# Edge attention: who normalises the four row tiles of a group, VectorE and GpSimd or VectorE alone

## The chip, the cores and the metric

The kernel runs on one core of a Trainium2 chip. The time is that of the device for the whole program, in microseconds (us). The core's engines work side by side, each through its own list of instructions in order, and hand over by semaphores: TensorE multiplies and transposes, VectorE and ScalarE work on rows in the on-chip memories SBUF and PSUM, GpSimd does elementwise work on SBUF, and SyncE issues the DMAs.

## The reference

A network of four layers over 128 graphs of 64 nodes with 256 features, each of the form x + layer(relu(layernorm(x))): graph convolutions with LSTMs over windows, an attention over 512 edges, a two-stage convolution with batch norm, a dense attention. The change lies in the second, the attention over edges. What it computes, cut:

```python
h = maximum(layernorm(x, axis=-1), 0)                 # (128, 64, 256), eps 1e-5
Xq = (h @ W_lin.T).reshape(bt, n, heads, dh)          # 4 heads of 64
Xv = (h @ W_val.T).reshape(bt, n, heads, dh)
e = einsum('behd,hd->beh', leaky_relu(Xq[:, src] + Xq[:, dst], 0.2), a)
e = e + log(adj[src, dst] + 1e-8)
attn = softmax of e over the edges with the same src
Y = segment_sum(attn[..., None] * Xv[:, dst], src)
x = x + Y @ W_out.T
```

The layernorm's first step is what the change touches: (x - mean) * (variance + eps) ** -0.5 for each row.

## The kernel before

The 8192 rows (graph and node) lie on 128 partitions in 16 groups of 4 row tiles of 128 rows each (GT = 4). `edge_attention` (L940) handles them in 4 quarters of 4 groups; q counts quarters, m groups in one, and G = 4q + m is the group's number, 0 to 15. Each engine's program is written out by hand in the order of a common schedule: `group(q, m)` has 8 steps i, one for each graph of group m, and in them the work for the next group (`project`, `split_hi`, `split_lo`) and for the one after that, n = m + 2, is done ahead: the transposes back to rows (`turn_back`, i = 0), x1 = x + h (`add_x`), the statistics (`measure`, i = 0, and `moments`, i = 1), the normalisation (`normalise`, i = 3), the transposes of the normalised rows (`turn`, i = 5). The code for quarter 0 is unrolled, the middle two are a loop, the last is cut short. Groups 0, 1 and 2 are prepared in the opening and in `group(0, 0)`.

The normalisation before the change: VectorE leaves mean and variance of every row in c_mv and variance + eps in c_ve (L1496, semaphore var_eps). GpSimd takes that to the power -0.5 (L1092, c_rstd, semaphore rstd_ready). Then VectorE normalises the tiles 0 and 1 (NT = 2) with one tensor_scalar each (L1503), and GpSimd the tiles 2 and 3 with a subtraction (L1096) and a multiplication (L1099) over both. Each adds one to the semaphore normed, and TensorE's `turn` (L1154) waits for both. In the trace these rows are named l_w and x1 is l_x. The last thing in VectorE's step 3, behind `normalise`, is `split_lo` (L1532, L1535), which copies the values and writes the low halves of c_keys out of the PSUM bank c_pU; TensorE may write the next projection (`project`, L53 to L55) into c_pU only then. Beside that, `gather` (L1193) and `score` (L1208) are TensorE's other work in a group.

GpSimd has a second task in this phase: `make_pairs` (L1106) multiplies the one-hot tables of sources and destinations into edge_pairs, in eight instructions of 2048 elements for each partition. Three stand behind group 2's share of the normalisation, once VectorE has made the tables (`one_hot_columns`, L1719 and L1720, just ahead of `normalise(0, 2)`), and five behind group 3's. VectorE's `edge_cuts` (L1707 to L1710) stands in step 6 of `group(0, 0)`, after the first three are under way.

Of the kernel before, what the change touches and what calls it, by code (L numbers as in the profile page):

```python
# [8 lines left out]
ALU = mybir.AluOpType  # L9
# [3 lines left out]
P = 128  # L13
BATCH, NODES, D = 128, 64, 256
# [3 lines left out]
GT = 4  # L18
# [20 lines left out]
def wait(eng, sem, value):  # L39

    if isinstance(value, int) and value <= 0:
        return
    eng.wait_ge(sem, value)
# [896 lines left out]
def edge_attention(core, x, x2, tables, h_rows, spilled, pairs, late):  # L940


    nc = core.nc
    NQ, QG, QT = 4, 32, 16
    GG = GT * TILE_GRAPHS
    NJ = QT // GT
    AHEAD = 2
    HG = GG // 2
    NH = QG // HG
    NT = 2  # L950
    with ExitStack() as ctx:
        sb, ps = allocator(nc, ctx)
        tab = tables.tab
# [2 lines left out]
        xt, hst, landed = late.x, late.w, late.landed  # L956
        st, mv, ve, rstd = sb("c_st", [P, GT, 6]), sb("c_mv", [P, GT, 2]), sb("c_ve", [P, GT]), sb("c_rstd", [P, GT])
# [38 lines left out]
        sem = {n: core.sem("c_" + n) for n in names}  # L996
# [23 lines left out]
        with nc.Block() as block:  # L1020
# [62 lines left out]
            @block.gpsimd  # L1083
            def _(pool):
                nc.gpsimd.memset(mhalf[:, :], -0.5).then_inc(sem["half_set"], 1)
                nc.gpsimd.memset(lin[:, :], 0.0).then_inc(sem["half_set"], 1)
                pool.wait_ge(sem["half_set"], 2)

                def normalise(q, m):
                    G = NJ * q + m  # L1090
                    pool.wait_ge(sem["var_eps"], G + 1)
                    nc.gpsimd.tensor_tensor(rstd[:, :], ve[:, :], mhalf[:, :], ALU.pow).then_inc(sem["rstd_ready"], 1)  # L1092
                    pool.wait_ge(sem["rstd_ready"], 2 * G + 1)
                    xn = hst[m % 2][:, :, :].rearrange("p k (a d) -> p (k a) d", d=D)
                    shape = [P, GT - NT, D]
                    nc.gpsimd.tensor_tensor(xn[:, NT:, :], xt[m % 2][:, NT:, :],  # L1096
                                            mv[:, NT:, 0:1].to_broadcast(shape), ALU.subtract).then_inc(sem["rstd_ready"], 1)
                    pool.wait_ge(sem["rstd_ready"], 2 * G + 2)
                    nc.gpsimd.tensor_tensor(xn[:, NT:, :], xn[:, NT:, :], rstd[:, NT:].unsqueeze(2).to_broadcast(shape),  # L1099
                                            ALU.mult).then_inc(sem["normed"], 1)  # L1100

                def make_pairs(first, end):
                    for n in range(first, end):
                        c, half = n // 2, slice(n % 2 * NODES // 2, (n % 2 + 1) * NODES // 2)
                        shape = [P, NODES // 2, NODES]
                        nc.gpsimd.tensor_tensor(pairs[:, c, :].rearrange("p (i j) -> p i j", j=NODES)[:, half, :],  # L1106
                                                tab["src"][:, c, half].unsqueeze(2).to_broadcast(shape),
                                                tab["dst"][:, c, :].unsqueeze(1).to_broadcast(shape),
                                                ALU.mult).then_inc(sem["pairs_made"], 1)

                def body(q, last=False):
                    for m in range(3, NJ if last else NJ + 3):
                        normalise(q, m)
                        if isinstance(q, int) and q == 0 and m == 3:
                            make_pairs(3, NP)

                normalise(0, 0)
                normalise(0, 1)
                normalise(0, 2)
                pool.wait_ge(spilled[0], 16)  # L1120
                pool.wait_ge(spilled[1], 16 * (SPILLS - 1))
                pool.wait_ge(tables.made, ONE_HOT)
                make_pairs(0, 3)
                body(0)
                with pool.Fori(1, NQ - 1) as q:
                    body(q)
                body(NQ - 1, last=True)
                pool.wait_ge(late.opened["var_eps"], 1)
                nc.gpsimd.tensor_tensor(late.rs[:, :], late.ve[:, :], mhalf[:, :], ALU.pow).then_inc(late.opened["rstd_ready"], 1)

            @block.tensor
            def _(pe):
# [14 lines left out]

                def turn(q, m):

                    pe.wait_ge(sem["normed"], 2 * (NJ * q + m + 1))  # L1150
                    xn = hst[m % 2][:, :, :].rearrange("p k (a d) -> p (k a) d", d=D)
                    for t in range(GT):
                        for k in range(KD):
                            last = nc.tensor.transpose(pT[:, k, t * P:(t + 1) * P], xn[:, t, k * P:(k + 1) * P],  # L1154
                                                       tab["ident"][:, :])
                    last.then_inc(sem["t2"], 1)
# [312 lines left out]
            def _(dve):  # L1469
# [8 lines left out]
                def measure(q, m):  # L1478
                    G = NJ * q + m
                    dve.wait_ge(sem["x1_done"], G + 1)  # L1480
                    wait(dve, sem["rstd_ready"], 2 * G)
                    V.memset(ve[:, :], EPS)
                    for t in range(GT):
                        last = V.bn_stats(st[:, t, :], xt[m % 2][:, t, :])
                    last.then_inc(sem["stats"], 1)

                def moments(q, m):
                    G = NJ * q + m
                    dve.wait_ge(sem["stats"], 2 * G + 1)
                    wait(dve, sem["normed"], 2 * G)  # L1490
                    V.memset(unused[:, :], 0.0)
                    for t in range(GT):
                        last = V.bn_aggr(mv[:, t, :], st[:, t, :])
                    last.then_inc(sem["stats"], 1)
                    dve.wait_ge(sem["stats"], 2 * G + 2)
                    V.tensor_tensor(ve[:, :], ve[:, :], mv[:, :, 1], ALU.add).then_inc(sem["var_eps"], 1)  # L1496

                def normalise(q, m):
                    G = NJ * q + m
                    dve.wait_ge(sem["rstd_ready"], 2 * G + 1)  # L1500
                    xn = hst[m % 2][:, :, :].rearrange("p k (a d) -> p (k a) d", d=D)
                    for t in range(NT):
                        last = V.tensor_scalar(xn[:, t, :], xt[m % 2][:, t, :], mv[:, t, 0:1],  # L1503
                                               rstd[:, t:t + 1], ALU.subtract, ALU.mult)
                    last.then_inc(sem["normed"], 1)
# [244 lines left out]
def attention_layer(core, x, x2, h_rows, spilled, pairs, tables, late):  # L1750
    with ExitStack() as ctx:
        sb, _ = allocator(core.nc, ctx)
        sb("t_tables", [P, Tables.BYTES // 4])
        edge_attention(core, x, x2, tables, h_rows, spilled, pairs, late)
# [839 lines left out]
```

## Time and profile before

| | us |
|---|---|
| median of three runs | 2063.58 |
| lowest and highest | 2061.97, 2063.68 |
| span of the profiled execution | 2060.7 |
| TensorE busy | 1967.9 |
| VectorE busy | 1255.3 |
| ScalarE busy | 1000.0 |
| GpSimd busy | 224.2 |

Of the profiled execution the span from the first to the last instruction is known; its own device time isn't listed apart from the three runs. An engine's busy time is the sum of its instructions' durations. The names of tiles are those of the program: c_ for the edge attention, t_ for its tables, l_ for buffers that later phases share. A group that reads "x2" stands for two instructions, with the time from the start of the first to the end of the second; in brackets stands how long the engine had been idle before, and which instruction ended that.

### The profile page before, as it was taken

How to read it: one execution, taken by the hardware profiler on the slowest of the kernel's cores; microseconds unless marked ns; L12 is line 12 of the kernel's file. 1: busy time of each engine (PE TensorE's matmuls, PEld its weight loads, DVE VectorE, ACT ScalarE, POOL GpSimd, SP SyncE). 2: the span in 40 equal slices, each digit the busy share in tenths (PEclk: the TensorE clock that was granted, in tenths of full speed). 3: DMA queues.
4: the chain of work that ended last, by engine and by line, in shares of the span. 5: the costliest groups of instructions: out<-in, count | busy, mean ns of one | idle time of the engine just before them, and what ended most of it. 6: DMA issues, size and time to landing. Idle time of an engine off the chain costs nothing. (4 is left out here: it accounts for less than half of the span.)

```text
span 2060.7 us, 33850 instructions
## 1 busy us (share of the span) xinstructions
PE 1967.9 (95%) x12438; PEld 1632.4 (79%) x12438; DVE 1255.3 (61%) x2629; ACT 1000.0 (49%) x1675; POOL 224.2 (11%) x202
## 2 busy tenths in 40 slices
PE   6999999999999999999999889999999899897998
PEld 6998888888899999888888556757566688686998
DVE  7454665454455545555653776565664488897786
ACT  2554664333333433323332464462636246575996
POOL 1000000100110111011011350010100011100000
PEclk9999999999999999999999999999999999998999
DMA  3101001000100000101002321422314032001232
GB/s 118 56 27 41 0 0 41 0 0 0 41 1 0 0 0 0 31 1 41 41 0 82 133 72 52 145 83 85 112 36 151 12 113 71 23 0 52 82 103 92
DMA packets 81486, 99.92 MB, mean 48 GB/s; under 512 B 7408, under 2 KB 73584, under 8 KB 79088
## 3 DMA queue, kind: packets, MB, share of 16 engines
q1 hardware_dynamic: 81392, 98.65, 14.6%
q8 instruction: 61, 1.00, 0.2%
q14 instruction: 33, 0.27, 0.0%
HBM read 61.78 MB, written 33.55 MB: 46 GB/s over the span
## 5 line engine op out<-in xcount | busy, mean ns | idle before, releaser
L703 ACT ACTIVATE b_gate<-b_pG,b_bias 128x512 f32<-128x512 f32 (+1 forms) x504 | 303.9, 633 | 356.5 <-PE b_pG L55 355.6
L53 PE MATMUL b_pG<-b_xshi,b_whi 128*128 128x512 f32 (+1 forms) x1008 | 366.7, 364 | 2.2 <-PEq L299 1.4
L55 PE MATMUL b_pG<-b_xshi,b_wlo 128*128 128x512 f32 (+1 forms) x1008 | 366.1, 363 | 0.0
L54 PE MATMUL b_pG<-b_xslo,b_whi 128*128 128x512 f32 (+1 forms) x1008 | 366.1, 363 | 0.0
L753 DVE CAST b_xshi<-HT 128x512 fp32r<-128x512 f32 (+3 forms) x142 | 58.9, 457 | 284.4 <-PE b_pG L55 267.7
L53 PEld LDWEIGHTS b_pG<-b_xshi,b_whi 128*128 128x128 f32 x1008 | 189.2, 188 | 29.2 <-issue 3.5
L54 PEld LDWEIGHTS b_pG<-b_xslo,b_whi 128*128 128x128 f32 x1008 | 189.2, 188 | 25.7
L55 PEld LDWEIGHTS b_pG<-b_xshi,b_wlo 128*128 128x128 f32 x1008 | 189.2, 188 | 25.4
L55 PE MATMUL b_pG<-b_hshi,b_wlo 128*128 128x512 f32 (+1 forms) x576 | 205.1, 356 | 0.0
L54 PE MATMUL b_pG<-b_hslo,b_whi 128*128 128x512 f32 (+1 forms) x576 | 205.1, 356 | 0.0
L53 PE MATMUL b_pG<-b_hshi,b_whi 128*128 128x512 f32 (+1 forms) x576 | 205.1, 356 | 0.0
L711 ACT ACTIVATE b_tc<-b_cell 128x512 f32<-128x512 f32 (+1 forms) x144 | 83.7, 581 | 213.6 <-DVE b_cell L897 111.7
L724 POOL TENSOR_TENSOR b_gate<-b_gate 128x512 f32<-128x512 f32 (+1 forms) x72 | 83.2, 1156 | 924.6 <-ACT b_gate L703 924.6
L1400 ACT ACTIVATE c_relu<-c_pZ 128x512 f32<-128x512 f32 x256 | 138.3, 596 | 37.4 <-PE c_pZ L1193 36.3
L53 PEld LDWEIGHTS b_pG<-b_hshi,b_whi 128*128 128x128 f32 x576 | 108.1, 188 | 12.6
L54 PEld LDWEIGHTS b_pG<-b_hslo,b_whi 128*128 128x128 f32 x576 | 108.1, 188 | 12.5
L55 PEld LDWEIGHTS b_pG<-b_hshi,b_wlo 128*128 128x128 f32 x576 | 108.1, 188 | 12.3
L757 DVE TENSOR_TENSOR b_xslo<-HT,b_xshi 128x512 fp32r<-128x512 f32 (+1 forms) x142 | 100.1, 746 | 2.4
L901 DVE TENSOR_TENSOR HT<-b_gate,b_tc 128x512 f32 (+3 forms) x72 | 51.8, 720 | 66.5 <-ACT b_tc L711 66.5
L1193 PE MATMUL c_pZ<-t_both,c_keys 128*128 128x512 f32 x256 | 86.9, 423 | 0.0
L1193 PEld LDWEIGHTS c_pZ<-t_both,c_keys 128*128 128x128 f32 x256 | 42.1, 188 | 46.8 <-issue 33.5
L904 DVE TENSOR_TENSOR b_tc<-b_gate,b_tc 128x512 f32<-128x512 f32 (+1 forms) x72 | 44.0, 611 | 54.7 <-ACT b_tc L711 54.7
(366 smaller groups left out, 3975.8 us busy)
## 6 DMA issues: line engine op xcount, KB each, us to landing
a_xt<-in_x SPq DMA_DIRECT2D x16, 512.0 KB, 5.6
h_scratch<-HT SPq DMA_DIRECT2D x4, 2048.0 KB, 7.6
l_x<-in_x SPq DMA_DIRECT2D x16, 512.0 KB, 4.0
l_w<-h_scratch SPq DMA_DIRECT2D x16, 512.0 KB, 5.1
x_scratch<-l_x SPq DMA_DIRECT2D x16, 512.0 KB, 3.2
c_x<-x_scratch SPq DMA_DIRECT2D x32, 256.0 KB, 3.9
x_scratch<-c_x SPq DMA_DIRECT2D x32, 256.0 KB, 2.9
l_x<-x_scratch SPq DMA_DIRECT2D x16, 512.0 KB, 3.8
```

The source lines that it names most:

```text
L53: nc.tensor.matmul(out, w_hi, x_hi, start=first, stop=False)
L54: nc.tensor.matmul(out, w_hi, x_lo, start=False, stop=False)
L55: return nc.tensor.matmul(out, w_lo, x_hi, start=False, stop=last)
L703: nc.scalar.activation(gate[s][:, g, 0:plan.n], pG[s][:, g, 0:plan.n], SIG[g], bias=bias[:, plan.p - 1, 2 * g + s:2 * g + s + 1])\
L711: nc.scalar.activation(tc[s][:, 0:plan.n], cell[b][:, s, 0:plan.n], ACT.Tanh).then_inc(tanh_ready, 1)
L724: nc.gpsimd.tensor_tensor(gate[s][:, I, 0:plan.n], gate[s][:, I, 0:plan.n], gate[s][:, G, 0:plan.n], ALU.mult).then_inc(ig_ready, 1)
L753: nc.vector.tensor_copy(plan.flat(xs_hi[b][:, k, :]), plan.windows(it, b, k, t))\
L757: last = nc.vector.tensor_tensor(plan.flat(xs_lo[b][:, k, :]), plan.windows(it, b, k, t), plan.flat(f32(xs_hi[b][:, k, :])), ALU.subtract)
L901: nc.vector.tensor_tensor(plan.windows(it, b, s, t), plan.flat(gate[s][:, O, :]), plan.flat(tc[s][:, :]), ALU.mult).then_inc(h_ready, 1)
L904: nc.vector.tensor_tensor(tc[s][:, 0:n], gate[s][:, O, 0:n], tc[s][:, 0:n], ALU.mult).then_inc(h_ready, 1)
L1193: nc.tensor.matmul(pZ[i % 2][:, k, :], keys[:, i, k * P:(k + 1) * P], tab["both"][:, :], start=True, stop=True).then_inc(sem["z_mm"], 1)
L1400: nc.scalar.activation(relu_rows[i % RB][:, k, :], pZ[i % 2][:, k, :], ACT.Relu).then_inc(sem["r_done"], 1)
```

## The change

All four tiles are normalised by VectorE, with four tensor_scalar instructions in place of two. GpSimd keeps the power alone; its subtraction and multiplication (2 x 16 instructions) go. The counts of the semaphores are adapted: normed and rstd_ready rise by one for each group instead of two. GpSimd's function gets one more wait, for the rows of the group before (normed), since the power overwrites c_rstd, which the normalisation reads.

```diff
--- before.py
+++ after.py
@@ -947,7 +947,6 @@
     AHEAD = 2
     HG = GG // 2
     NH = QG // HG
-    NT = 2
     with ExitStack() as ctx:
         sb, ps = allocator(nc, ctx)
         tab = tables.tab
@@ -1086,18 +1085,11 @@
                 nc.gpsimd.memset(lin[:, :], 0.0).then_inc(sem["half_set"], 1)
                 pool.wait_ge(sem["half_set"], 2)
 
-                def normalise(q, m):
+                def root(q, m):
                     G = NJ * q + m
                     pool.wait_ge(sem["var_eps"], G + 1)
+                    wait(pool, sem["normed"], G)
                     nc.gpsimd.tensor_tensor(rstd[:, :], ve[:, :], mhalf[:, :], ALU.pow).then_inc(sem["rstd_ready"], 1)
-                    pool.wait_ge(sem["rstd_ready"], 2 * G + 1)
-                    xn = hst[m % 2][:, :, :].rearrange("p k (a d) -> p (k a) d", d=D)
-                    shape = [P, GT - NT, D]
-                    nc.gpsimd.tensor_tensor(xn[:, NT:, :], xt[m % 2][:, NT:, :],
-                                            mv[:, NT:, 0:1].to_broadcast(shape), ALU.subtract).then_inc(sem["rstd_ready"], 1)
-                    pool.wait_ge(sem["rstd_ready"], 2 * G + 2)
-                    nc.gpsimd.tensor_tensor(xn[:, NT:, :], xn[:, NT:, :], rstd[:, NT:].unsqueeze(2).to_broadcast(shape),
-                                            ALU.mult).then_inc(sem["normed"], 1)
 
                 def make_pairs(first, end):
                     for n in range(first, end):
@@ -1110,13 +1102,13 @@
 
                 def body(q, last=False):
                     for m in range(3, NJ if last else NJ + 3):
-                        normalise(q, m)
+                        root(q, m)
                         if isinstance(q, int) and q == 0 and m == 3:
                             make_pairs(3, NP)
 
-                normalise(0, 0)
-                normalise(0, 1)
-                normalise(0, 2)
+                root(0, 0)
+                root(0, 1)
+                root(0, 2)
                 pool.wait_ge(spilled[0], 16)
                 pool.wait_ge(spilled[1], 16 * (SPILLS - 1))
                 pool.wait_ge(tables.made, ONE_HOT)
@@ -1147,7 +1139,7 @@
 
                 def turn(q, m):
 
-                    pe.wait_ge(sem["normed"], 2 * (NJ * q + m + 1))
+                    pe.wait_ge(sem["normed"], NJ * q + m + 1)
                     xn = hst[m % 2][:, :, :].rearrange("p k (a d) -> p (k a) d", d=D)
                     for t in range(GT):
                         for k in range(KD):
@@ -1478,7 +1470,7 @@
                 def measure(q, m):
                     G = NJ * q + m
                     dve.wait_ge(sem["x1_done"], G + 1)
-                    wait(dve, sem["rstd_ready"], 2 * G)
+                    wait(dve, sem["rstd_ready"], G)
                     V.memset(ve[:, :], EPS)
                     for t in range(GT):
                         last = V.bn_stats(st[:, t, :], xt[m % 2][:, t, :])
@@ -1487,7 +1479,7 @@
                 def moments(q, m):
                     G = NJ * q + m
                     dve.wait_ge(sem["stats"], 2 * G + 1)
-                    wait(dve, sem["normed"], 2 * G)
+                    wait(dve, sem["normed"], G)
                     V.memset(unused[:, :], 0.0)
                     for t in range(GT):
                         last = V.bn_aggr(mv[:, t, :], st[:, t, :])
@@ -1497,9 +1489,9 @@
 
                 def normalise(q, m):
                     G = NJ * q + m
-                    dve.wait_ge(sem["rstd_ready"], 2 * G + 1)
+                    dve.wait_ge(sem["rstd_ready"], G + 1)
                     xn = hst[m % 2][:, :, :].rearrange("p k (a d) -> p (k a) d", d=D)
-                    for t in range(NT):
+                    for t in range(GT):
                         last = V.tensor_scalar(xn[:, t, :], xt[m % 2][:, t, :], mv[:, t, 0:1],
                                                rstd[:, t:t + 1], ALU.subtract, ALU.mult)
                     last.then_inc(sem["normed"], 1)
```

On GpSimd, at the place where the pairs are made (between the powers of group 2, group 3 and group 4). Before:

```order
L1092 TENSOR_TENSOR c_rstd<-c_ve,c_mhalf 128x4 [waits c_var_eps]
L1096 TENSOR_TENSOR l_w_52<-l_x_50,c_mv 128x512 [waits c_rstd_ready]
L1099 TENSOR_TENSOR l_w_52<-l_w_52,c_rstd 128x512 [waits c_rstd_ready]
L1106 TENSOR_TENSOR edge_pairs<-t_src,t_dst 128x2048 [waits t_made,h_spilled_rest,h_spilled_first]
L1106 TENSOR_TENSOR edge_pairs<-t_src,t_dst 128x2048 x2
L1092 TENSOR_TENSOR c_rstd<-c_ve,c_mhalf 128x4 [waits c_var_eps]
L1096 TENSOR_TENSOR l_w_53<-l_x_51,c_mv 128x512 [waits c_rstd_ready]
L1099 TENSOR_TENSOR l_w_53<-l_w_53,c_rstd 128x512 [waits c_rstd_ready]
L1106 TENSOR_TENSOR edge_pairs<-t_src,t_dst 128x2048 x5
```

Now, with the powers of groups 1 and 2 ahead and those of groups 4 to 6 behind:

```order
L1092 TENSOR_TENSOR c_rstd<-c_ve,c_mhalf 128x4 [waits c_normed,c_var_eps] x2
L1098 TENSOR_TENSOR edge_pairs<-t_src,t_dst 128x2048 [waits t_made,h_spilled_rest,h_spilled_first]
L1098 TENSOR_TENSOR edge_pairs<-t_src,t_dst 128x2048 x2
L1092 TENSOR_TENSOR c_rstd<-c_ve,c_mhalf 128x4 [waits c_normed,c_var_eps]
L1098 TENSOR_TENSOR edge_pairs<-t_src,t_dst 128x2048 x5
L1092 TENSOR_TENSOR c_rstd<-c_ve,c_mhalf 128x4 [waits c_normed,c_var_eps] x3
```

The pairs stand directly behind a power, and the five of the second batch have no wait of their own.

On VectorE, from the last one-hot tables to the end of step 3 of `group(0, 0)`, with group 2's normalisation. Before:

```order
L1719 TENSOR_SCALAR t_src<-s_iota_row,s_s_col 128x64
L1720 TENSOR_SCALAR t_dst<-s_iota_row,s_d_col 128x64
L1503 TENSOR_SCALAR l_w_52<-l_x_50,c_mv,c_rstd 128x256 [waits c_rstd_ready]
L1503 TENSOR_SCALAR l_w_52<-l_x_50,c_mv,c_rstd 128x256
L1532 COPY c_vals<-c_pU 128x256 [waits c_s_hi]
L1535 TENSOR_TENSOR c_keys<-c_pU,c_keys 64x256 x2
```

Now:

```order
L1711 TENSOR_SCALAR t_src<-s_iota_row,s_s_col 128x64
L1712 TENSOR_SCALAR t_dst<-s_iota_row,s_d_col 128x64
L1495 TENSOR_SCALAR l_w_52<-l_x_50,c_mv,c_rstd 128x256 [waits c_rstd_ready]
L1495 TENSOR_SCALAR l_w_52<-l_x_50,c_mv,c_rstd 128x256 x3
L1524 COPY c_vals<-c_pU 128x256 [waits c_s_hi]
L1527 TENSOR_TENSOR c_keys<-c_pU,c_keys 64x256 x2
```

Four instructions with one wait ahead of them stand where two stood; what follows is the same.

## Rows read from the trace of the kernel before

**Rows 1.** The page: the span, and TensorE's busy time, weight loads apart.

```profile
span 2060.7 us, 33850 instructions
PE 1967.9 (95%) x12438; PEld 1632.4 (79%) x12438; DVE 1255.3 (61%) x2629; ACT 1000.0 (49%) x1675; POOL 224.2 (11%) x202
```

**Rows 2.** A window: stretch, its us, PE busy (instructions), granted clock, DMA share, GB/s.

```profile
1160.00:1600.00 440.00, 416.01 (x3628) 1.00 0.28 91
```

**Rows 3.** PE's waits, 1130 to 1680: for whom, total us, times, longest us.

```profile
PE c_pT L1154 <- DVE l_w L1503: 9.7, 15, 2.7
```

**Rows 4.** The timeline of a regular group: start us, us, engine, line, operation.

```profile
1338.43 1.01 POOL L1092 TENSOR_TENSOR c_rstd<-c_ve,c_mhalf 128x4 f32<-128x4 f32 x1 [15.67 <-DVE c_ve L1496]
...
1339.47 2.35 DVE L1503 TENSOR_SCALAR l_w<-l_x,c_mv,c_rstd 128x256 f32<-128x256 f32 x2 [1.12 <-POOL c_rstd L1092]
...
1339.52 1.04 POOL L1096 TENSOR_TENSOR l_w<-l_x,c_mv 128x512 f32<-128x512 f32 x1
...
1340.63 1.04 POOL L1099 TENSOR_TENSOR l_w<-l_w,c_rstd 128x512 f32<-128x512 f32 x1
...
1340.83 0.73 PE L1193 MATMUL c_pZ<-t_both,c_keys 128*128 128x512 f32 x2
...
1341.88 1.09 PE L1154 MATMUL c_pT<-t_ident,l_w 128*128 128x128 f32 x8 [0.31 <-DVE l_w L1503]
...
1343.21 0.50 PE L53 MATMUL c_pU<-t_wqv_hi,c_hThi 128*128 128x512 f32 x1 [0.23 <-DVE c_keys L1535]
```

**Rows 5.** The timeline of group 0's normalisation, with GpSimd idle beside it.

```profile
1146.34 0.74 DVE L1503 TENSOR_SCALAR l_w<-l_x,c_mv,c_rstd 128x256 f32<-128x256 f32 x2
...
1146.67 0.41 DVE L1503 TENSOR_SCALAR l_w<-l_x,c_mv,c_rstd 128x256 f32<-128x256 f32 x1
```

**Rows 6.** The timeline: TensorE where it waits for nothing.

```profile
1188.43 0.71 PE L1193 MATMUL c_pZ<-t_both,c_keys 128*128 128x512 f32 x2
...
1202.05 0.74 PE L1193 MATMUL c_pZ<-t_both,c_keys 128*128 128x512 f32 x2
1202.63 0.40 PE L53 MATMUL c_pU<-t_wqv_hi,c_hThi 128*128 128x512 f32 x1
```

**Rows 7.** The timeline: transposes of a group with a softmax scan, one of three.

```profile
1257.60 1.09 PE L1154 MATMUL c_pT<-t_ident,l_w 128*128 128x128 f32 x8 [1.19 <-DVE l_w L1503]
```

**Rows 8.** The timeline: the pairs on GpSimd, and VectorE's instructions beside them.

```profile
1175.50 7.26 POOL L1106 TENSOR_TENSOR edge_pairs<-t_src,t_dst 128x2048 fp32r<-128x2048 f32 x2
...
1180.92 2.38 DVE L1709 TENSOR_TENSOR t_cut<-c_work 128x511 f32<-128x511 f32 x1
...
1182.72 4.06 POOL L1106 TENSOR_TENSOR edge_pairs<-t_src,t_dst 128x2048 fp32r<-128x2048 f32 x1
...
1183.34 3.73 DVE L1710 TENSOR_SCALAR t_cut<-t_cut 128x513 f32<-128x513 f32 x1
...
1196.58 18.00 POOL L1106 TENSOR_TENSOR edge_pairs<-t_src,t_dst 128x2048 fp32r<-128x2048 f32 x5
...
1212.01 2.59 DVE L1496 TENSOR_TENSOR c_ve<-c_ve,c_mv 128x4 f32<-128x4 f32 x1
```

**Rows 9.** The timeline of VectorE: normalisation of group 2 and of group 3.

```profile
1173.27 0.25 DVE L1720 TENSOR_SCALAR t_dst<-s_iota_row,s_d_col 128x64 f32<-128x64 f32 x1
1173.43 2.26 DVE L1503 TENSOR_SCALAR l_w<-l_x,c_mv,c_rstd 128x256 f32<-128x256 f32 x2
...
1194.42 2.35 DVE L1503 TENSOR_SCALAR l_w<-l_x,c_mv,c_rstd 128x256 f32<-128x256 f32 x2 [1.12 <-POOL c_rstd L1092]
```

**Rows 10.** The timeline of TensorE: behind edge_cuts, and the transposes of group 4.

```profile
1187.61 1.06 PE L1144 MATMUL c_pT<-t_ident,l_w 128*128 128x128 f32 x8 [2.06 <-DVE c_lin L1523]
...
1218.13 1.09 PE L1154 MATMUL c_pT<-t_ident,l_w 128*128 128x128 f32 x8 [2.74 <-DVE l_w L1503]
```

**Rows 11.** Windows of PE where the attention opens, columns as in Rows 2.

```profile
1132.00:1136.00 4.00, 0.36 (x2) 0.88 0.00 0
...
1136.50:1142.50 6.00, 5.54 (x19) 0.55 0.94 377
1142.50:1144.50 2.00, 1.94 (x17) 1.00 0.53 183
```

## The prediction

> **What bounds the kernel now.** I read the page first, then the stretch in which the changed code runs, then its single instructions. On the page TensorE is busy 1967.9 us of a span of 2060.7 [rows 1], and in the steady part of the edge attention, 1160 to 1600 us, 416.0 of 440.0 us at full clock [rows 2]. So the time changes only where TensorE waits, or where its waits get longer. The list of its waits names one that the change touches directly: L1154, the transposes that take the normalised rows, waited 9.7 us in 15 places, 2.7 us at the longest [rows 3].
>
> A regular group [rows 4] shows why. GpSimd's power starts at 1338.43 and takes 1.01 us. VectorE starts its two row tiles at 1339.47 and takes 2.35 us for both; GpSimd's subtraction and multiplication run beside them, 1.04 us each, until 1341.67. TensorE starts the transposes at 1341.88 (0.31 us idle), and L53, the next projection, at 1343.21 (0.23 us idle), when VectorE has also done the L1532 and L1535 that queued behind its normalisation. Undisturbed, two such VectorE instructions take 0.74 us, the first 0.41 and each further one 0.33 [rows 5]. Here each lasts some 1.2 us and ends about 0.15 us behind one GpSimd instruction: VectorE is held up until GpSimd's current instruction is through.
>
> **What the change takes away.** In a regular group four instructions alone take 0.41 + 3 x 0.33 = 1.40 us instead of 2.35, so the rows, and then c_keys, are ready 0.95 us earlier. What can TensorE use of that? The gather L1193 ahead of the transposes starts at 1340.83 [rows 4], and where nothing waits the next matrix starts 0.58 us after a gather (1202.05 to 1202.63, [rows 6]); a block of eight transposes holds TensorE for 0.82 us (1187.61 to 1188.43, [rows 6, 10]). So the transposes could start at 1341.41 and L53 at 1342.23, while c_keys allows it at 1342.26; it starts at 1343.21 now. That is 0.95 us if the modelled starts are right; the idle times alone, 0.31 + 0.23, give 0.54. In the three groups where a softmax scan delays the power (1.19 us idle, [rows 7], and 0.23 behind it), VectorE sets the pace throughout and its 0.95 us count whole. I take 0.9 us for each of the groups 5 to 15, numbered from 0: 11 x 0.9 = 9.9 us; the least is 8 x 0.54 + 3 x 0.95 = 7.2. Groups 0 and 1 lie in the opening, where the 0.74 us of group 0 become 1.40 while an instruction ahead of it is no longer held up; I put both at nothing, give or take 0.7 us. The wait that GpSimd gets, for the rows of the group before, is met long before: it had stood idle 15.67 us ahead of its power [rows 4].
>
> **What the change moves: the pairs.** Twice GpSimd has other work behind its power: L1106 builds edge_pairs, three instructions behind group 2 and five behind group 3, 3.6 us each [rows 8]. Before, they stood behind GpSimd's share of the normalisation. Now they stand directly behind the power, and VectorE's four instructions meet them. How does VectorE fare beside them? Three places say [rows 8]. L1709 (two inputs in SBUF) was issued at 1180.92 while the second pair instruction ran until 1182.76, and ended at 1183.30. L1710, a tensor_scalar like the normalisation, was issued at 1183.34, met the third one (1182.72, lasting 4.06 us to 1186.78) and ended at 1187.07. L1496, on four columns, took 2.59 us and ended with the fifth of the second batch. So one VectorE instruction waits for one GpSimd instruction to end, gets in between two of them, and the next waits again. That queued ones don't slip through together is seen in [rows 4]: the two normalising instructions have no wait between them, and yet the second ended 0.15 us behind GpSimd's second instruction (1341.82 against 1341.67), not 0.33 us behind the first.
>
> Group 3: the power ends just before 1194.4, and the first pair instruction, which waits for nothing more, is ahead of VectorE, which started at 1194.42 [rows 9]. Four instructions wait for four pair instructions, 4 x 3.6 = 14.4 us: rows ready at 1194.35 + 14.4 + 0.15 = 1208.9 instead of 1194.42 + 2.35 = 1196.77. L1532 and L1535 and with them the next projection queue behind, so that all of it falls on TensorE. **+12.1.**
>
> Group 2: the pairs also wait for the one-hot tables, which VectorE finishes at 1173.52; its first normalising instruction is issued at 1173.43 [rows 9], so it should be ahead of the first pair instruction (1173.60). The second, third and fourth wait for three pair instructions: 1173.75 + 3 x 3.6 + 0.2 = 1184.8, against 1175.69. **+9.1.** If two get ahead it is 5.5.
>
> Two waits go. edge_cuts (L1709, L1710) took 6.1 us between the pairs, and TensorE stood idle 2.06 us before L1144 [rows 10], counted from the gather's end, 0.15 us after the next matrix could have started; now edge_cuts run when the first three pairs are over: **-2.2**. And group 4's power, which stood behind the fifth pair instruction as L1496 did, let the transposes start at 1218.13 after 2.74 us idle [rows 10], the longest of the waits, 2.43 more than in a regular group; TensorE comes 19 us later by then and the pairs do not. With the 0.95 of a regular group: **-3.4**.
>
> **The clock.** Two stalls of 9 and 12 us may let the clock fall. The nearest rows: between the LSTM and the attention TensorE was busy 0.36 of 4 us at a granted clock of 0.88, and in the six us behind it, in which it worked 5.54, the clock was 0.55, that is half speed (1.2 GHz) for 90% of them; the two us after that had it full [rows 11]. So behind a restart up to 5.4 us of work go at half speed, a loss of 2.7 us for each stall; from below the bound is nothing. I take 2.0 twice, nearer to the row, since these idle times are longer than that one: **+4**.
>
> The Trainium skill (SBUF — State Buffer, Who interferes with whom) says that the shared port pair is locked for a full instruction, that the loser blocks fully, and that whoever issues first gets it. The trace agrees with the first two (2.59 us for L1496); on the third, VectorE was issued 0.05 us ahead at 1339.47 and was held up all the same. By that rule VectorE's second instruction of group 2, due at 1173.76, stands behind the pair instruction of 1173.60, which gives the 9.1 and not the 5.5.
>
> **Sum.** 12.1 + 9.1 - 2.2 - 3.4 - 9.9 + 4 = +9.7 us. The profiled execution has a span of 2060.7 us; its own total isn't given, and the median is 2.9 us above the span, so I carry the difference to the median: 2063.6 + 9.7 = **2073.3 us**.
>
> **The rivals.** A (15%), the other side: once VectorE has the port its queued instructions run through, and GpSimd's next one waits. It is decided at the gap between two pair instructions. For it: L1709 did get in between two that had no wait between them. Against it: [rows 4]. Price: group 2 gains 0.8 us, since all four come ahead of the pairs; group 3 waits for one pair instruction, 1194.35 + 3.6 + 0.15 + 3 x 0.33 = 1199.1, +2.3; edge_cuts meet the pairs as before, so their 2.2 us stay; no stall is long enough for the clock: -0.8 + 2.3 - 3.4 - 9.9 = -11.8, **2051.8 us**. B (9%): VectorE's instructions don't get in until a batch is over. Group 2 ends at 1184.4 + 1.0, +9.7; group 3 at 1212.35 + 1.4, +17.0; the rest as forecast: 9.7 + 17.0 - 2.2 - 3.4 - 9.9 + 4 = +15.2, **2078.8 us**. L1709 between two pair instructions speaks against it. C (8%): in group 2 two instructions get ahead of the pairs, 5.5 instead of 9.1: **2069.7 us**. That the change doesn't do what it says can be left out: in the order of the instructions GpSimd has none left on l_w, and VectorE has a block of four.
>
> **Chances and range.** Forecast 68%, A 15%, B 9%, C 8%. C with the clock at nothing gives 2065.7, and with the opening's 0.7 and the spread of the runs some 2063; B with the clock at its dearest and the smallest gain gives 2083, of which I take in 2081. The range of 2063 to 2081 leaves out A and little else. Within 0.2% (4.1 us, about what a measurement of this kernel can tell from no change) lie the edge of C and of the forecast without a clock loss: 8%. Faster 15%, slower 77%.
>
> **What would show it.** Right: group 3's four VectorE instructions last 3.6 us each and end one by one behind the pair instructions, with TensorE idle some 12 us before the transposes; group 2 the same with three; a clock of 0.5 behind both; regular groups 0.9 us shorter, without idle time before L1154; nothing left of the 2.74 us of group 4. A would show one long instruction and three of 0.4 us, B one that is as long as the batch. If the regular groups keep their length, the 9.9 us are the wrong step; if the stalls are there but the clock stays full, the 4 us are.

## The result and the profile after

The changed kernel takes 2070.86 us (median of 5 runs, 2068.66 to 2072.05) against 2063.58 before: ratio 1.0038, 95% interval [1.0028, 1.0049], so it is slower by 7.3 us. The forecast was +9.7 us and a range of 2063 to 2081. Two later series of the same kernel gave 1.0030 [1.0018, 1.0042] and 1.0044 [1.0030, 1.0057].

The page, which answers [rows 1]: TensorE works as long as before, in a span that is 6.4 us longer, and GpSimd's 33.5 us of subtractions and multiplications are gone. VectorE is busy 2.9 us longer: its blocks are shorter in most groups and much longer in two. An instruction that is held up counts as busy.

```profile
span 2067.1 us, 33849 instructions
PE 1966.7 (95%) x12438; PEld 1636.2 (79%) x12438; DVE 1258.2 (61%) x2661; ACT 1000.1 (48%) x1675; POOL 190.7 (9%) x170
```

The list of TensorE's waits, 1130 to 1690 us, against [rows 3] (waiting instruction, for whom, total us, times, longest us). Fifteen waits with 9.7 us in total have become six with 23.6, and the longest, 2.7 us before, is now 12.5:

```profile
PE c_pT L1146 <- DVE l_w L1495: 23.6, 6, 12.5
```

A regular group, against [rows 4]. The normalisation's four tiles take 1.38 us, the transposes L1146 (before: L1154) and L53 start without idle time, and the next power starts 17.90 us after this one, where it took 18.91 before:

```profile
1351.88 1.01 POOL L1092 TENSOR_TENSOR c_rstd<-c_ve,c_mhalf 128x4 f32<-128x4 f32 x1 [16.90 <-DVE c_ve L1488]
...
1352.92 1.38 DVE L1495 TENSOR_SCALAR l_w<-l_x,c_mv,c_rstd 128x256 f32<-128x256 f32 x4 [1.12 <-POOL c_rstd L1092]
...
1354.27 0.73 PE L1185 MATMUL c_pZ<-t_both,c_keys 128*128 128x512 f32 x2
...
1354.84 1.03 PE L1146 MATMUL c_pT<-t_ident,l_w 128*128 128x128 f32 x8
1355.68 0.50 PE L53 MATMUL c_pU<-t_wqv_hi,c_hThi 128*128 128x512 f32 x1
...
1369.78 1.01 POOL L1092 TENSOR_TENSOR c_rstd<-c_ve,c_mhalf 128x4 f32<-128x4 f32 x1 [16.89 <-DVE c_ve L1488]
```

The groups 2 and 3 beside the pairs, against [rows 8 to 10], from the timelines of VectorE, GpSimd and TensorE in the order of time. VectorE's blocks of four last 11.28 and 14.57 us, where the blocks of two lasted 2.26 and 2.35; TensorE stands idle 9.35 and 12.55 us before the transposes, which then take 1.97 us for eight instead of 1.09:

```profile
1173.12 11.28 DVE L1495 TENSOR_SCALAR l_w<-l_x,c_mv,c_rstd 128x256 f32<-128x256 f32 x4
...
1173.37 10.87 POOL L1098 TENSOR_TENSOR edge_pairs<-t_src,t_dst 128x2048 fp32r<-128x2048 f32 x3 [0.38 <-DVE t_dst L1712]
...
1184.45 1.97 PE L1146 MATMUL c_pT<-t_ident,l_w 128*128 128x128 f32 x8 [9.35 <-DVE l_w L1495]
...
1191.16 0.69 DVE L1701 TENSOR_TENSOR t_cut<-c_work 128x511 f32<-128x511 f32 x1
1191.89 0.43 DVE L1702 TENSOR_SCALAR t_cut<-t_cut 128x513 f32<-128x513 f32 x1
...
1202.45 18.12 POOL L1098 TENSOR_TENSOR edge_pairs<-t_src,t_dst 128x2048 fp32r<-128x2048 f32 x5
...
1202.52 14.57 DVE L1495 TENSOR_SCALAR l_w<-l_x,c_mv,c_rstd 128x256 f32<-128x256 f32 x4 [1.12 <-POOL c_rstd L1092]
...
1217.14 1.97 PE L1146 MATMUL c_pT<-t_ident,l_w 128*128 128x128 f32 x8 [12.55 <-DVE l_w L1495]
...
1236.31 1.03 PE L1146 MATMUL c_pT<-t_ident,l_w 128*128 128x128 f32 x8
```

Single instructions, from short windows of the same timelines. In group 2 the first of the four is ahead of the pairs and takes 0.40 us; the second is held up and takes 3.71. In group 3 the first ends 0.15 us behind the first pair instruction (1206.22 against 1206.07). The last of the four starts at 1213.39, takes 3.70 us too, and ends 0.15 us behind the fourth pair instruction (1209.66 + 7.28 = 1216.94). GpSimd itself loses little by this: its five instructions take 18.12 us, against 18.00 before, where one VectorE instruction met them:

```profile
1173.12 0.40 DVE L1495 TENSOR_SCALAR l_w<-l_x,c_mv,c_rstd 128x256 f32<-128x256 f32 x1
...
1173.44 3.71 DVE L1495 TENSOR_SCALAR l_w<-l_x,c_mv,c_rstd 128x256 f32<-128x256 f32 x1
...
1202.45 3.62 POOL L1098 TENSOR_TENSOR edge_pairs<-t_src,t_dst 128x2048 fp32r<-128x2048 f32 x1
1202.52 3.70 DVE L1495 TENSOR_SCALAR l_w<-l_x,c_mv,c_rstd 128x256 f32<-128x256 f32 x1 [1.12 <-POOL c_rstd L1092]
...
1209.66 7.28 POOL L1098 TENSOR_TENSOR edge_pairs<-t_src,t_dst 128x2048 fp32r<-128x2048 f32 x2
...
1213.39 3.70 DVE L1495 TENSOR_SCALAR l_w<-l_x,c_mv,c_rstd 128x256 f32<-128x256 f32 x1
```

Not everything on VectorE is held up. Before the change the second batch of pairs ran from 1196.58 to 1214.58. Beside it the copy out of PSUM (L1532, 0.42 us), the sum of a PSUM and an SBUF tile (L1476, 1.22) and the first of the statistics (L1484, 0.42) took as long as elsewhere, and L1496, with both inputs in SBUF, took 2.59 us instead of 0.16.

Windows of TensorE, columns as in [rows 11] (stretch, us, busy time with instructions, granted clock, DMA share, GB/s). In both stalls the clock falls to 0.50, 1.2 GHz, and is still there when work resumes:

```profile
1178.00:1182.00 4.00, 0.00 (x0) 0.61 0.00 0
1182.00:1186.00 4.00, 1.55 (x8) 0.50 0.00 0
1186.00:1190.00 4.00, 4.00 (x18) 0.61 0.57 159
1190.00:1194.00 4.00, 4.00 (x32) 1.00 0.27 103
...
1208.00:1212.00 4.00, 0.00 (x0) 0.70 0.00 0
1212.00:1216.00 4.00, 0.00 (x0) 0.50 0.00 0
1216.00:1220.00 4.00, 2.86 (x11) 0.52 0.00 0
1220.00:1224.00 4.00, 4.00 (x26) 1.00 0.78 262
```

Where the time went is best read at GpSimd's powers (L1092), one in each group in both kernels. Their starts, and how much later the changed kernel is:

| group | before, us | after, us | later by |
|---|---|---|---|
| 2 | 1172.29 | 1171.97 | -0.32 |
| 3 | 1193.38 | 1201.47 | +8.09 |
| 4 | 1214.68 | 1233.34 | +18.66 |
| 5 | 1233.54 | 1251.24 | +17.70 |
| 6 | 1253.30 | 1270.05 | +16.75 |
| 7 | 1319.52 | 1333.97 | +14.45 |
| 10 | 1377.16 | 1388.59 | +11.43 |
| 15 | 1564.21 | 1570.94 | +6.73 |
| end of span | 2060.7 | 2067.1 | +6.4 |

It loses 19.0 us between the powers of group 2 and group 4, and gives back 11.9 from there to group 15: about 1.0 us for each of the 11 groups 4 to 14, and more than that between the groups 6 and 7, which is explained below.

### The profile page after: what moved, and what is told of

Read it like the earlier page. It is cut to its first block and busy times, and to the rows that moved or that the text cites. A ratio compares the mean times of both kernels' runs of the same rounds, so it can differ in the third digit from the quotient of the medians.

```text
span 2067.1 us, 33849 instructions
## 1 busy us (share of the span) xinstructions
PE 1966.7 (95%) x12438; PEld 1636.2 (79%) x12438; DVE 1258.2 (61%) x2661; ACT 1000.1 (48%) x1675; POOL 190.7 (9%) x170
## 5 line engine op out<-in xcount | busy, mean ns | idle before, releaser
L53 PE MATMUL b_pG<-b_xshi,b_whi 128*128 128x512 f32 (+1 forms) x1008 | 366.7, 364 | 2.2 <-PEq L299 1.4
L53 PEld LDWEIGHTS b_pG<-b_xshi,b_whi 128*128 128x128 f32 x1008 | 189.2, 188 | 29.3 <-issue 3.7
L53 PE MATMUL b_pG<-b_hshi,b_whi 128*128 128x512 f32 (+1 forms) x576 | 205.1, 356 | 0.0
L55 PEld LDWEIGHTS b_pG<-b_hshi,b_wlo 128*128 128x128 f32 x576 | 108.1, 188 | 12.5
L53 PEld LDWEIGHTS b_pG<-b_hshi,b_whi 128*128 128x128 f32 x576 | 108.1, 188 | 12.5
L54 PEld LDWEIGHTS b_pG<-b_hslo,b_whi 128*128 128x128 f32 x576 | 108.1, 188 | 12.4
L1185 PEld LDWEIGHTS c_pZ<-t_both,c_keys 128*128 128x128 f32 x256 | 42.4, 190 | 47.0 <-issue 33.5
```

What stands on the lines that cost most here:

```text
L53: nc.tensor.matmul(out, w_hi, x_hi, start=first, stop=False)
L54: nc.tensor.matmul(out, w_hi, x_lo, start=False, stop=False)
L55: return nc.tensor.matmul(out, w_lo, x_hi, start=False, stop=last)
L1185: nc.tensor.matmul(pZ[i % 2][:, k, :], keys[:, i, k * P:(k + 1) * P], tab["both"][:, :], start=True, stop=True).then_inc(sem["z_mm"], 1)
```

## The experiments

The theory to be tested: the change saves 1 us in every group, since VectorE no longer takes turns with GpSimd in the normalisation, and loses more than that in two groups, since its four instructions now take turns with the pairs. The rivals: that four instructions in a row on VectorE or the new wait on GpSimd cost something by themselves; that each VectorE instruction waits for something else than one GpSimd instruction; that the loss behind the stalls is not the clock. The times of one series are compared with runs of the kernel before on the same chip.

### The pairs wait for the rows

```diff
                         root(q, m)
                         if isinstance(q, int) and q == 0 and m == 3:
+                            pool.wait_ge(sem["normed"], 4)
                             make_pairs(3, NP)
...
+                pool.wait_ge(sem["normed"], 3)
                 make_pairs(0, 3)
```

> The changed kernel, but GpSimd starts each batch of pairs only when VectorE has finished the rows of that group (a wait for normed ahead of the three and ahead of the five). If the two stalls come from VectorE's four instructions taking turns with the pairs (my theory), both go: no idle time of 9 and 12 us before the transposes, full clock, and the time falls by 9.0 + 12.2 for the stalls and some 3.5 for the clock; edge_cuts meet the pairs again (2 us of idle time before the transposes back come back) and the power of group 4 stands behind the fifth pair instruction again (2.5 us come back). Near 2051 us. Rival: the new wait on GpSimd or the longer VectorE block makes the loss, then moving the pairs changes little and the time stays near 2070.

Measured: 2052.12 us, ratio 0.9948 [0.9934, 0.9962]. VectorE's block, from its timeline in this kernel, is 1.37 and 1.38 us in the groups 2 and 3, and TensorE's idle times are the two that were expected:

```profile
1172.82 1.37 DVE L1497 TENSOR_SCALAR l_w<-l_x,c_mv,c_rstd 128x256 f32<-128x256 f32 x4
...
1193.23 1.38 DVE L1497 TENSOR_SCALAR l_w<-l_x,c_mv,c_rstd 128x256 f32<-128x256 f32 x4 [1.12 <-POOL c_rstd L1092]
```

```profile
1186.42 1.06 PE L1138 MATMUL c_pT<-t_ident,l_w 128*128 128x128 f32 x8 [2.37 <-DVE c_lin L1517]
...
1215.22 1.15 PE L1148 MATMUL c_pT<-t_ident,l_w 128*128 128x128 f32 x8 [2.02 <-DVE l_w L1497]
```

Two waits more on GpSimd turn a kernel that is 7 us slower than before into one that is 11 us faster. The stalls come from the meeting with the pairs; neither four instructions in a row on VectorE nor a wait on GpSimd is the cause. The expectation of a full clock was missed at one place: behind the second of these idle times the granted clock was 0.77 in 1214 to 1218 and 0.81 in 1218 to 1222, and from the power of group 4 to that of group 5 it took 19.28 us instead of 17.9.

### The pairs spread behind the rows of the groups 3 and 4

```diff
-                        if isinstance(q, int) and q == 0 and m == 3:
-                            make_pairs(3, NP)
+                        if isinstance(q, int) and q == 0 and m in (3, 4):
+                            pool.wait_ge(sem["normed"], m + 1)
+                            make_pairs(4 * (m - 3), 4 * (m - 2))
...
-                make_pairs(0, 3)
```

> The changed kernel, with the eight pair instructions as four behind the rows of group 3 and four behind those of group 4, each batch in the 15 us between a normalisation and the next statistics, where VectorE has nothing that shares the port. By my theory neither the normalisation nor edge_cuts nor the power of group 4 meets a pair instruction: 2.2 for edge_cuts, 2.4 for group 4, 1.0 us for each of 13 or 14 groups: some 18 us less than before, near 2046 us, faster than both kernels. Rival: the pairs delay VectorE wherever they stand, then it stays above 2055.

> The changed kernel with the pairs spread behind the rows of groups 3 and 4 once more, since its runs lay 5 us apart: 2042 to 2045 us, ratio 0.990.

Measured: 2042.04 us, ratio 0.9898 [0.9883, 0.9913], and again 2042.82 us, 0.9906 [0.9889, 0.9922]. It is faster than both kernels, by 1% against the one before, and no wait of TensorE for l_w is left among its longer ones. GpSimd's timeline shows the batch that ends 1 us before the next power is wanted:

```profile
1194.10 14.37 POOL L1098 TENSOR_TENSOR edge_pairs<-t_src,t_dst 128x2048 fp32r<-128x2048 f32 x4 [1.50 <-DVE l_w L1495]
1209.50 1.01 POOL L1092 TENSOR_TENSOR c_rstd<-c_ve,c_mhalf 128x4 f32<-128x4 f32 x1 [1.03 <-DVE c_ve L1488]
```

It came 4 us lower than expected. In the second trace 373.54 us lie between the powers of group 2 and group 15, where the trace of the kernel before has 391.92: 18.4 less, of which 1.5 are a stretch of low clock in the latter (below). Where the rest of the 20 us between the medians lies isn't shown. The difference of the two profiled executions of this kernel, 2044.8 and 2041.6 us, is told below.

### The kernel before, with the same spread

The same edit of `body` and the same line removed, in the kernel before, where the count to wait for is `2 * (m + 1)`.

> The kernel before, with nothing changed but the place of the pairs: four behind the rows of group 3, four behind those of group 4. This is the part of the gain that has nothing to do with who normalises: edge_cuts no longer meet the pairs (2.2 us) nor does the power of group 4 (2.4 us): 4.6 us less than before, near 2059 us. Regular groups stay 18.9 us apart. The difference to the changed kernel with the same spread is what the normalisation on VectorE alone is worth, 13 us by my theory. Rival: if the pairs cost nothing before, 2063.6.

Measured: 2056.97 us, ratio 0.9967 [0.9956, 0.9978]. From the power of group 2 to that of group 4 it takes 1211.03 - 1173.23 = 37.80 us instead of 42.39, which is the 4.6 us expected: 2.17 us less from group 2 to group 3, where edge_cuts were, and 2.42 less from group 3 to group 4. The median is 2 us lower than the 2059 expected. Its groups stay 18.9 us apart:

```profile
1211.03 1.01 POOL L1092 TENSOR_TENSOR c_rstd<-c_ve,c_mhalf 128x4 f32<-128x4 f32 x1 [1.03 <-DVE c_ve L1496]
...
1212.08 2.35 DVE L1503 TENSOR_SCALAR l_w<-l_x,c_mv,c_rstd 128x256 f32<-128x256 f32 x2 [1.12 <-POOL c_rstd L1092]
...
1229.91 1.01 POOL L1092 TENSOR_TENSOR c_rstd<-c_ve,c_mhalf 128x4 f32<-128x4 f32 x1 [1.03 <-DVE c_ve L1496]
```

So the normalisation on VectorE alone is worth 2056.97 - 2042.8 = 14 us where it meets nothing (13.4 by the ratios, since the two ran on different chips). Between the powers of group 2 and group 15 the traces differ by 385.94 - 373.54 = 12.4 us, 0.95 for each of 13 groups.

### Three tiles on VectorE, one on GpSimd

The kernel of the run above with `NT = 3`.

> The kernel before with NT = 3: VectorE normalises three tiles, GpSimd one (two instructions of 256 elements); the pairs are spread behind the rows of groups 3 and 4. If VectorE loses a turn to each GpSimd instruction and nothing else, its block takes two turns of some 0.6 to 0.7 us and one free instruction of 0.33, 1.6 to 1.8 us: between the 2.35 of two tiles and the 1.40 of four. The groups are then about 0.3 us longer than with four tiles, 4 us for the 13 groups: 2050 us where four tiles with spread pairs give 2046. If the length of the block didn't count, it would equal that kernel.

Measured: 2050.17 us, ratio 0.9935 [0.9921, 0.9948]. The block takes 1.82 us and the groups are 18.4 us apart, 0.5 us more than with four tiles where 0.3 was expected; the whole is 7 us slower than with four tiles instead of 4. Its timeline shows two instructions held up by two shorter ones of GpSimd, and the third free:

```profile
1210.10 1.82 DVE L1503 TENSOR_SCALAR l_w<-l_x,c_mv,c_rstd 128x256 f32<-128x256 f32 x3 [1.12 <-POOL c_rstd L1092]
...
1210.14 0.61 POOL L1096 TENSOR_TENSOR l_w<-l_x,c_mv 128x256 f32<-128x256 f32 x1
1210.84 0.61 POOL L1099 TENSOR_TENSOR l_w<-l_w,c_rstd 128x256 f32<-128x256 f32 x1
```

2.35, 1.82 and 1.38 us for the block give 18.9, 18.4 and 17.9 us for the group. The more tiles VectorE takes, the shorter its block, since the time that it no longer loses to GpSimd's instructions is more than the further tiles take.

### The pairs in halves

```diff
-                        shape = [P, NODES // 2, NODES]
...
+                        shape = [P, NODES // 4, NODES]
+                        for part in range(2):
+                            rows = slice(half.start + part * NODES // 4, half.start + (part + 1) * NODES // 4)
...
```

Each of the two multiplies its 16 rows of the pairs; the place of the batches is that of the changed kernel.

> The changed kernel, with each pair instruction cut into two of half the size, in the same place. If VectorE gets in once between any two GpSimd instructions, each of its instructions waits for one of some 1.85 us: the block of group 3 takes 7.3 us instead of 14.6, that of group 2 some 5.7 instead of 11.3, so 12.9 us less stall and 1 to 3 us less clock loss: 2055 to 2058 us. If VectorE had to wait for time or for a batch (rival), the blocks keep their 11 and 14.6 us and the time its 2070.9.

Measured: 2056.10 us, ratio 0.9966 [0.9955, 0.9977]. The blocks are 6.12 and 7.70 us long, in VectorE's timeline:

```profile
1173.11 6.12 DVE L1497 TENSOR_SCALAR l_w<-l_x,c_mv,c_rstd 128x256 f32<-128x256 f32 x4
...
1196.71 7.70 DVE L1497 TENSOR_SCALAR l_w<-l_x,c_mv,c_rstd 128x256 f32<-128x256 f32 x4 [1.12 <-POOL c_rstd L1092]
```

GpSimd's ten instructions of the second batch take 18.84 us, 1.88 each, and four of them are 7.5 us. The elements that both engines work on are the same as in the changed kernel; GpSimd's instructions are half as long and twice as many, and the stall is half as long. A wait for a whole batch or for a fixed time is ruled out.

### Two large instructions on VectorE instead of four

```diff
-                    for t in range(GT):
-                        last = V.tensor_scalar(xn[:, t, :], xt[m % 2][:, t, :], mv[:, t, 0:1],
-                                               rstd[:, t:t + 1], ALU.subtract, ALU.mult)
-                    last.then_inc(sem["normed"], 1)
+                    shape = [P, GT, D]
+                    V.tensor_tensor(xn, xt[m % 2][:, :, :], mv[:, :, 0:1].to_broadcast(shape), ALU.subtract).then_inc(sem["centred"], 1)
+                    dve.wait_ge(sem["centred"], G + 1)
+                    V.tensor_tensor(xn, xn, rstd[:, :].unsqueeze(2).to_broadcast(shape), ALU.mult).then_inc(sem["normed"], 1)
```

> The changed kernel, but VectorE normalises the four tiles with two instructions of 1024 elements (subtract the mean, multiply by the root) instead of four of 256. If a turn is lost for each VectorE instruction, whatever its size, group 3's block loses two turns instead of four: 2 x 3.6 + 2 x 1.1 = 9.4 us instead of 14.6, and group 2's one turn: 1.2 + 3.6 + 1.1 = 5.9 instead of 11.3. Regular blocks take 2.4 us instead of 1.38, as long as in the kernel before, so those 11 us of gain go. Sum: 2070 - 5.2 - 5.4 + 11 - some clock = about 2069. Rival: if VectorE waits for the port for as long as GpSimd has pairs in its queue, or for a time that grows with the elements, the blocks stay at 11 and 14 us or more, and the time is 2080.

Measured: 2075.37 us, ratio 1.0057 [1.0040, 1.0073]. The blocks are as the theory has them, 5.8 and 9.2 us: one instruction is held up in group 2 and two in group 3.

```profile
1178.50 1.22 DVE L1495 TENSOR_TENSOR l_w<-l_x,c_mv 128x1024 f32<-128x1024 f32 x1
1179.75 4.53 DVE L1497 TENSOR_TENSOR l_w<-l_w,c_rstd 128x1024 f32<-128x1024 f32 x1
...
1201.51 4.64 DVE L1495 TENSOR_TENSOR l_w<-l_x,c_mv 128x1024 f32<-128x1024 f32 x1 [1.12 <-POOL c_rstd L1092]
1206.18 4.52 DVE L1497 TENSOR_TENSOR l_w<-l_w,c_rstd 128x1024 f32<-128x1024 f32 x1
```

The time expected for the whole, 2069 us, was missed by 6: the power of group 2 starts at 1177.36, 5.4 us later than in the changed kernel. I had put the opening at nothing. There the groups 0 and 1 are normalised with nothing to hide the longer block, and the trace of this kernel has the clock at 0.50 from 1150 to 1158. How the 5.4 us divide between the two isn't shown. The turns are confirmed, the sum was incomplete.

### TensorE kept busy in the stalls

```diff
+                    if isinstance(q, int) and q == 0 and m in (2, 3):
+                        pe.wait_ge(sem["x1_done"], m + 1)
+                        for _ in range(70 if m == 2 else 100):
+                            nc.tensor.transpose(pT[:, 0, 0:P], tab["ident"][:, :], tab["ident"][:, :])
                     pe.wait_ge(sem["normed"], NJ * q + m + 1)
```

> The changed kernel, but TensorE transposes the identity into the free bank 70 times ahead of the wait of group 2 and 100 times ahead of that of group 3, so that it is busy for most of the two stalls. It waits for the same rows at the same time. If the clock's fall costs 3.5 us, as the changed kernel's trace suggests (2.2 behind group 2, 1.3 behind group 3), the clock stays full and the time falls by that, to 2067.4 us. If the slow matrices behind the stalls are not the clock, nothing changes; if the transposes outlast the stall, it gets slower.

Measured: 2066.41 us, ratio 1.0019 [1.0010, 1.0028], some 3 us under the changed kernel by the ratios of its two series up to then (1.0038 and 1.0030). But the trace doesn't bear that out: from the power of group 2 to that of group 4 it takes 60.45 us where the changed kernel takes 61.37, 0.9 less, and behind the first stall, where TensorE had been without work for 1.72 us, the granted clock was 0.59 in 1186 to 1190. So this run proved little, and the number of transposes was raised.

> The changed kernel with 84 and 114 transposes of the identity ahead of the two waits, 14 more each than in the run with 70 and 100, whose transposes ended 1.7 us before the rows were ready and behind whose first stall the clock still fell for 3.4 us. Now TensorE idles for 0.1 to 0.2 us only. If idle time makes the clock fall, it is full behind both stalls, and from the transposes of the rows to the next score it takes 3.4 us both times, where the changed kernel takes 5.05 and 4.16: 2.5 us less in this stretch. The whole time then lies 2.5 us under that of the changed kernel; what it lies lower than that comes from the clock in other places. Rival: the clock goes by something else, and a low stretch remains.

> The changed kernel again, beside the run with 84 and 114 transposes on the same chip: 2070 us, ratio 1.0035, 2.5 us more than that run.

Measured on one chip: 2065.86 us, 1.0012 [1.0003, 1.0021], with the 84 and 114 transposes, and 2072.08 us, 1.0044 [1.0030, 1.0057], without. TensorE's timeline with them, and two windows:

```profile
1176.04 9.33 PE L1145 MATMUL c_pT<-t_ident 128*128 128x128 f32 x84
1185.58 1.09 PE L1150 MATMUL c_pT<-t_ident,l_w 128*128 128x128 f32 x8 [0.20 <-DVE l_w L1499]
...
1188.94 1.06 PE L1204 MATMUL c_pE<-c_relu,t_sign 128*32 128x512 f32 x8
```

```profile
1185.00:1190.00 5.00, 4.56 (x32) 1.00 0.42 130
...
1217.00:1222.00 5.00, 4.76 (x32) 1.00 0.60 198
```

The clock is full behind both stalls. From the transposes of the rows to the next score it takes 3.36 and 3.38 us, where the changed kernel takes 5.05 and 4.16, as expected. From power 2 to power 4 it takes 58.97 us, against 61.37, 61.53 and 62.85 in the three traces of the changed kernel. So idle TensorE does make the clock fall here, and that costs 2.4 to 3.9 us in this stretch. The medians differ by 6.2 us, so 2 to 4 us lie beyond the stretch. The spans of the two executions profiled on this chip differ by 5.3 us (2070.2 and 2064.9). Of these, 3.9 lie in the stretch and 1.5 between the powers of group 10 and group 11, where only the trace without the added transposes has a low clock (0.66 in 1432 to 1436); 1.1 lie behind the power of group 15, and 1.2 go the other way ahead of the power of group 1. For the medians the rest stays open.

The changed kernel's second series, for the comparisons above:

> The changed kernel once more, for the comparison with the other kernels on this chip: 2070.9 us, ratio 1.0035.

Measured: 2069.56 us, ratio 1.0030 [1.0018, 1.0042], with the same blocks of 11.28 and 14.57 us.

## Why the prediction was right

- **The turns** (+12.1 and +9.1). Measured 14.57 - 2.35 = 12.2 and 11.28 - 2.26 = 9.0 us. In group 2 one instruction was ahead of the pairs, in group 3 none, as forecast. The half pairs show that it is one GpSimd instruction for one of VectorE, and the waits ahead of the pairs that nothing else is in these terms. Rivals A, B and C fall: the blocks would have been 1.4 and 4.7 us with A, with B 12.0 and 19.3, and the first 7.7 with C.
- **The waits that go** (-2.2 and -3.4). edge_cuts took 1.16 us (1191.16 to 1192.32) instead of 6.1, with no idle time before the transposes back, and group 4's transposes start at 1236.31 with none. The kernel before with the pairs spread isolates both, without the regular gain: 2.17 and 2.42 us, against 2.2 and 2.43.
- **The regular groups** (-9.9, 0.9 each). Measured 18.91 to 17.90, 1.0, in a regular group, and 0.81 and 0.87 in the groups 10 and 14, two of the three with a softmax scan. There the power ends later, VectorE's block of two was only 2.28 us long before (1255.26, group 6), and the forecast had taken the full 0.95. From the power of group 5 to that of group 15, ten groups, it is 9.5 us without the low clock that is told under **What the sum didn't hold**; what group 15 gains can't be read apart. The modelled starts were the right ones to go by, not the idle times (0.54), and the term was right.
- **The clock** (+4). The step was right that it falls, and mis-sized. In the trace of the changed kernel the two stretches behind the stalls take 1.7 and 0.8 us more than with full clock, 2.5 in all; the run with TensorE kept busy gives 2.4 to 3.9 for the traces at hand. I took the loss from a stretch in which TensorE had work all the time. Here the first 1.3 us behind the transposes' start are waited for anyway, for c_keys, so that part of the slow matrices was hidden behind VectorE's L1524 and L1527. Beside that the clock had already fallen during the stalls, and behind the second it was full again some 3 us after the restart (1.00 in 1220 to 1224).
- **What the sum didn't hold.** In the trace of the kernel before the clock is low at the end of the first quarter; in the changed kernel's trace the same place (1309 to 1313) has it full:

```profile
1294.00:1298.00 4.00, 2.93 (x31) 0.68 0.00 0
```

  From the power of group 6 to that of group 7 the kernel before takes 66.22 us and the changed one 63.92. The kernel before with the pairs spread, whose normalisation is that of the kernel before, takes 64.75 with a full clock. So 1.5 of the 2.30 us gained there are this low clock of one execution. That is chance, and no term of the change.
- **The sum.** 12.2 + 9.0 - 2.2 - 3.4 - 9.5 + 2.5 - 1.5 = +7.1 us. The changed kernel is also 0.3 us earlier at the power of group 2 and gains 0.3 behind that of group 15, which gives the 6.4 by which the spans differ, to a tenth. The medians differ by 7.3. The forecast's 9.7 was too high by 1.5 for the clock's term; against the spans, another 1.5 is the low clock of the kernel before.
- **The rule.** That the loser blocks for the full instruction (the Trainium skill, SBUF — State Buffer, Who interferes with whom): the trace agrees (3.70 us for an instruction that takes 0.41 alone). That whoever issues first gets it fits group 2, where VectorE started 0.25 us ahead; where it started 0.05 us ahead, at 1339.47 and in nine more groups of the kernel before, it was held up all the same. The trace shows starts and not when the port was asked for.

## What to carry to other kernels

An engine that shares a port is a resource of its own: before work is moved from GpSimd to VectorE, look at what GpSimd will do at that moment instead, and how long a single instruction of it is, since each VectorE instruction that needs the port may wait for one whole GpSimd instruction. Long GpSimd work that nobody waits for belongs behind a semaphore that says that VectorE is through; here two such waits turned 7 us of loss into 11 of gain, and a better place made it some 20. Small VectorE instructions beside large GpSimd ones are the dear case: each of the seven that met the pairs lost 3.3 us, and the whole change is worth 1 us in a group.

## What the runs showed of the hardware that was not expected

The granted clock dips in some executions and not in others, at the same place of the same kernel. The two profiled executions of the kernel with the pairs spread, both with these windows at the end of the second quarter, first one:

```profile
1404.00:1408.00 4.00, 2.93 (x59) 0.73 0.02 4
1408.00:1412.00 4.00, 4.00 (x81) 0.84 0.19 66
```

and then the other:

```profile
1404.00:1408.00 4.00, 2.93 (x88) 1.00 0.02 4
1408.00:1412.00 4.00, 4.00 (x87) 1.00 0.25 84
```

TensorE was busy for the same 2.93 of 4 us, and in the 4 us ahead for the same 3.30 at full clock. From the power of group 10 to that of group 11 the first takes 65.38 us and the second 63.91: such a dip costs 1.5 us. The three traces of the changed kernel show it too: 63.92 and 63.93 us between these powers in two, 65.36 in the third. Differences of 1 to 3 us between two single executions of this kernel are therefore no evidence for anything, and a saving of that size shows only in the stretch in which it arises.
